# Encoder-side keys of a decoder block: K leaves PSUM once as fp32 with its halves made on GpSimd, value products stand in pairs, and the units of a batch in a new order

## The reference, cut to what matters

```python
# x (32, 56, 128), ctx_1024 (32, 1500, 128), 16 heads of 8
x = _layernorm(x + _L0_attn_ref(x, ...), axis=-1)
# cross-attention, q = x, k = v = ctx_1024
qh = (q @ Wq.T + bq).reshape(bs, -1, H, DK).transpose(0, 2, 1, 3)
kh = (k @ Wk.T + bk).reshape(bs, -1, H, DK).transpose(0, 2, 1, 3)
vh = (v @ Wv.T + bv).reshape(bs, -1, H, DK).transpose(0, 2, 1, 3)
scores = jnp.einsum('bhqd,bhkd->bhqk', qh, kh) / math.sqrt(DK)
attn = jax.nn.softmax(scores, axis=-1)
out = jnp.einsum('bhqk,bhkd->bhqd', attn, vh)
x = _layernorm(x + concat @ Wo.T + bo, axis=-1)
x = _layernorm(x + _L0_ffn_ref(x, ...), axis=-1)
```

## Time and profile before

| | us |
|---|---|
| median of 3 runs | 888.73 (888.48 to 889.25) |
| the profiled execution | 889.02 |
| its span, first to last instruction | 887.2 |
| first score of body 0 | at 133.01 |
| first score of body 1 | at 155.57 |
| first score of body 30 | at 797.01 |
| first score of body 31 | at 819.62 |

### The profile page before, as it was taken

How to read it: one execution, slowest core, us unless ns; L and a number is a source line. 1 busy time by engine, 2 the same in 40 slices (tenths; PEclk the granted TensorE clock), 3 DMA queues, 4 the chain that set the end, 5 groups by cost and what they waited for, 6 DMA issues and landing times.

```text
span 887.2 us, 28853 instructions
## 1 busy us (share of the span) xinstructions
PE 825.6 (93%) x11074; PEld 534.8 (60%) x11074; DVE 692.8 (78%) x1245; ACT 559.0 (63%) x759; POOL 294.3 (33%) x170
## 2 busy tenths in 40 slices
PE   6788669999999999999999999999999999998884
PEld 3555426666666666666666666666666666666553
DVE  7767687778787878787878787878787878788498
ACT  4566517666666666666666666666666666666863
POOL 6010524333333333333333333333333333300263
PEclk9989959999999999999999999999999999999898
DMA  6000044333333333333333333333333332222001
GB/s 201 1 10 21 21 129 105 92 86 90 86 87 87 86 88 87 87 86 88 85 87 88 86 86 88 87 87 89 85 92 82 93 84 78 52 53 55 1 1 42
DMA packets 29864, 67.37 MB, mean 76 GB/s; under 512 B 8072, under 2 KB 13192, under 8 KB 29704
## 3 DMA queue, kind: packets, MB, share of 16 engines
q1 hardware_dynamic: 29832, 66.94, 28.7%
HBM read 27.50 MB, written 0.92 MB: 32 GB/s over the span
## 4 chain that ended last, share of the span: by engine, by line
PE 73%; DVE 15%; ACT 5%; issue 5%; DMA 1%; DVEq 0%; POOL 0%; ACTq 0%
PE psum L807 19%; PE psum L846 16%; PE psum L831 14%; PE psum L800 6%; PE psum L794 6%; DVE r_sb L1112 5%; PE psum L851 4%; ACT kh L594 2%; PE psum L722 2%; DVE kl L1091 2%; PE psum L820 2%; PE psum L708 1%; DVE k_stack L1226 1%; DVE rden L1025 1%; DVE mx L1098 1%
## 5 line engine op out<-in xcount | busy, mean ns | idle before, releaser
L1098 DVE TENSOR_REDUCE mx<-psum 128x1 f32<-128x500 f32 x672 | 413.0, 672 | 52.7 <-PE psum L807 49.5
L576 ACT ACTIVATE probs<-psum 125x896 f32<-125x896 f32 x384 | 352.7, 919 | 149.9 <-PE psum L831 146.4
L807 PE MATMUL psum<-kh,q_max 128*128 128x500 f16 x672 | 234.5, 383 | 7.3 <-DVE mx L1098 2.0
L831 PE MATMUL psum<-q_diag,k_stack 97*128 97x224 f16 x1536 | 212.9, 261 | 2.7 <-DMA q_diag<-mT 1.8
L846 PE MATMUL psum<-probs,v_ext 125*32 125x168 f32 x3072 | 189.3, 319 | 1.2 <-ACT probs L576 1.2
L831 PEld LDWEIGHTS psum<-q_diag,k_stack 97*128 97x128 f16 x1536 | 140.7, 98 | 46.6 <-issue 16.9
L442 POOL CAST c_hl<-c_in 128x1500 f16<-128x1500 f32 x32 | 45.9, 1434 | 267.8 <-PE psum L800 261.9
L1091 DVE SCALAR_TENSOR_TENSOR kl<-psum,pack,kh 128x500 f16<-128x500 f32 x96 | 68.0, 735 | 83.4 <-ACT kh L594 83.4
L846 PEld LDWEIGHTS psum<-probs,v_ext 125*32 125x32 f32 x3072 | 60.6, 108 | 114.9 <-issue 97.2
L450 POOL TENSOR_TENSOR q_diag<-q_stack,pack 96x896 f16<-96x896 f32 (+1 forms) x32 | 54.2, 1693 | 171.0 <-PE psum L831 158.7
L851 PE MATMUL psum<-probs,v_ext 125*16 125x56 f32 x3072 | 108.4, 213 | 0.0
(11 more groups left out here) (143 smaller groups left out, 735.0 us busy)
## 6 DMA issues: line engine op xcount, KB each, us to landing
c_in<-ctx_in SPq DMA_DIRECT2D x32, 750.0 KB, 4.3
k_stack<-kh SPq DMA_DIRECT2D x256, 93.8 KB, 2.2
k_stack<-kl SPq DMA_DIRECT2D x128, 93.8 KB, 2.2
pack<-pack_in SPq DMA_DIRECT2D x1, 1107.0 KB, 5.9
q_stack<-qh SPq DMA_DIRECT2D x32, 32.0 KB, 1.8
out<-x_all SPq DMA_DIRECT2D x8, 112.0 KB
pack<-pack_in SPq DMA_DIRECT2D x1, 848.5 KB, 4.7
x_all<-x_in SPq DMA_DIRECT2D x2, 336.0 KB
```

The source lines that it names most:

```text
L576: nc.scalar.activation(probs[0:KP, t % PBUF, :].rearrange("p (a c) -> p a c", a=2), scores[t % 2][0:KP, :, 0:2 * GC], ACT.Exp, scale=SCALE ...
L807: last = nc.tensor.matmul(bank[:, 0:CH], q_max[u][:, r * P:(r + 1) * P], kh[:, c * CH:(c + 1) * CH], start=True, stop=True)
L831: last = nc.tensor.matmul(scores[t % 2][:, g // 2, (g % 2) * GC:(g % 2 + 1) * GC], k_stack[u][0:ROWS, g, t * KP:t * KP + P], q_diag[u][0:R ...
L1098: dve.tensor_reduce(mx[:, i:i + 1], bank[:, 0:CH], AX.X, ALU.max).then_inc(mx_done, 1)
```

## The change

- **K.** ACT writes K of a chunk once as fp32 to a new buffer k32 (k_copy), which frees the bank. POOL casts it to kh (kcast) and subtracts for kl (ksub), chunk by chunk. DVE's k_lo is gone. kh and kl now exist twice (u = 0, 1). SP's stack_k waits for kl as before.
- **POOL's order.** split works in three chunks, and takes batch b+2 in body b. A body on POOL is now: cast of the last chunk of b+1, split of b+2, subtraction of that chunk, q_max, q_diag, then cast and subtraction of the first two chunks of b+2.
- **Value products.** They come two at a time, every second step, for the two steps before. The last two of a batch stand in the next body. The 224 columns are cut into 112 and 112 (v_ext's columns 0 to 32 and 16 to 48), so two heads in each product; WoSlots, selB and R follow.
- **Units.** PLAN gives for each pair of steps what stands after the first score, after the second, and after the two value products. K of a batch is made in three places: chunks 0 and 1 in body b-2 (K2), chunk 2 in body b-1 (K1). M goes chunk by chunk rather than row by row (M_ORDER): the first 7 (chunk 0) in body b-2 (M2), the other 14 in body b-1 (M1). R, and with it the reciprocal, moves from step 0 to step 7, X from step 11 to the end of step 7; o_copy of b-1 goes to DVE's place ahead of step 2.
- **Ends.** Two K and seven M of batch 1 are made ahead of body 0. The split of batch 1 stands early in POOL's front part. The last bodies have no K2 and M2.
- The scratch that the program reserves for DMA descriptors is set to 1024, for the new buffers' room.

The core of the diff:

```diff
-M_COUNTS = (2, 2, 3, 2, 3, 2, 3, 2, 2)
-V_STEPS, Y_STEP = (0, 2, 4), 6
-X_STEP = 11
-TAIL = [("K", c) for c in range(KC)]
+EARLY_M = 7
+PLAN = ((("M1",), ("M1", "K1", "M1"), ("V", "M1", "V")),
...
+O_COPY = (1, -1)
...
-                def split(n, buf, half):
+                def split(n, buf, half, i):
...
+                    keys = slice(i * CH, (i + 1) * CH)
+                    nc.gpsimd.tensor_copy(c_hl[:, buf, 0, keys], c_in[:, buf, keys]).then_inc(c_hi, 1)
...
+                def kcast(n, i, u):
...
+                    pool.wait_ge(k32_done, n * KC + i + 1)
                     settle(pool, pool_settled)
+                    nc.gpsimd.tensor_copy(kh[u][:, i * CH:(i + 1) * CH], k32[:, i * CH:(i + 1) * CH]).then_inc(kh_done, 1)
+
+                def ksub(n, i, u):
...
+                    nc.gpsimd.tensor_tensor(kl[u][:, keys], k32[:, keys], kh[u][:, keys],
+                                            ALU.subtract).then_inc(kl_done, 1)
...
-                def k_hi(n, i, bank):
...
+                def k_copy(n, i, bank):
+                    act.wait_ge(ready["K"], n * KC + i + 1)
+                    wait_past(act, kl_done, (n - 1) * KC + i + 1)
+                    nc.scalar.activation(k32[:, i * CH:(i + 1) * CH], bank[:, 0:CH], ACT.Identity,
+                                         bias=w("bk")).then_inc(k32_done, 1)
...
+                    elif kind in ("M1", "M2"):
+                        r, c = M_ORDER[i]
+                        if i % MB == 0:
+                            pe.wait_ge(kh_done, n * KC + c + 1)
...
-                        nc.tensor.matmul(O[32 * j:32 * j + 32, 0:3 * N], v_ext[u][0:KP, t, j, 0:32],
-                                         probs[0:KP, t % PBUF, at:at + 3 * N], start=(t == 0), stop=(t == KT - 1),
+                        nc.tensor.matmul(O[32 * j:32 * j + 32, 0:2 * N], v_ext[u][0:KP, t, j, 0:32],
+                                         probs[0:KP, t % PBUF, at:at + 2 * N], start=(t == 0), stop=(t == KT - 1),
...
+                    for m, (one, two, three) in enumerate(plans[u]):
+                        score(b, 2 * m, u)
...
+                        go(one)
+                        score(b, 2 * m + 1, u)
+                        go(two)
+                        if m:
+                            pv(b, 2 * m - 2, u)
+                            pv(b, 2 * m - 1, u)
+                        elif before:
+                            pv(b - 1, KT - 2, 1 - u)
+                            pv(b - 1, KT - 1, 1 - u)
+                        go(three)
...
-                def k_lo(n, i, bank):
...
-                    dve.scalar_tensor_tensor(kl[:, i * CH:(i + 1) * CH], bank[:, 0:CH], w("bk"),
-                                             kh[:, i * CH:(i + 1) * CH], ALU.add, ALU.subtract).then_inc(kl_done, 1)
```

More of the change, by code:

```diff
@@ L508, in add_b2 @@
+                for b in range(B - 2, B):
+                    body(b, b // 2, b % 2, False, b + 1 < B)
                 def add_b2(q):
@@ L782, in _, with release @@
                 front(QUADS - 1, True, False)
-                def unit(kind, i, n, u, bank, before):
+                def release(before):
                     if before is not None:
@@ new lines, in of_batch, with body, go @@
+                def of_batch(kind, b, pair):
+                    return {"K2": b + 2, "M2": b + 2, "R": b - 1, "Y": pair - 1}.get(kind, b + 1)
+                def body(b, pair, u, s1, s2, before, held):
+                    held = dict(held)
+                    def go(units):
+                        for kind, i in units:
+                            if active(kind, s1, s2, before):
+                                n, slot = of_batch(kind, b, pair), slots[u][kind, i]
+                                if kind in ("M1", "M2") and i in PAIRS:
+                                    release(held[slots[u][kind, i + 1]])
+                                unit(kind, i, n, u if kind in ("K2", "M2") else 1 - u, ring[slot], held[slot])
+                                held[slot] = (kind, i, n)
+                    for m, (one, two, three) in enumerate(plans[u]):
+                        score(b, 2 * m, u)
+                        if not s2 and 2 * m in X2T_STEPS:
+                            x2_T(X2T_STEPS.index(2 * m))
+                        go(one)
[8 more added lines that the diff above has]
+                        go(three)
+                    if not s2:
+                        pv(b, KT - 2, u)
+                        pv(b, KT - 1, u)
@@ L1145, in _ @@
                 q_lo(QUADS - 1)
[L1146 to L1147 removed]
+                for i in range(EARLY_M):
+                    m_max(1, i, banks[early_bank("M1", i)])
                 dve.wait_ge(sin_done, 1)
@@ L1198, in body @@
                                 add_y(pair - 1, bank)
-                    for i in range(KC):
-                        if s1:
-                            k_lo(b + 2, i, ring[slots[u]["K", i]])
-                        if i == 0:
-                            o_copy(b, u)
+                    for m, parts in enumerate(plans[u]):
+                        if (m, -1) == O_COPY and before and s2:
+                            o_copy(b - 1, 1 - u)
+                        for part, units in enumerate(parts):
+                            reduce(units)
+                            if (m, part) == O_COPY and before and s2:
+                                o_copy(b - 1, 1 - u)
                 for b in range(2):
```

305 lines of the change are left out of this document (166 added, 139 removed).

## The result

| | before | after |
|---|---|---|
| median, us | 888.85 (888.48 to 889.25) | 841.27 (839.2 to 841.89) |
| profiled execution | 889.02 | 840.91 |
| its span | 887.2 | 838.9 |
| first score of body 0 | 133.01 | 133.54 |
| of body 1 | 155.57 | 158.00 |

The changed kernel takes 0.9461 of the time before [0.9443, 0.9478], 47.6 us less, inside the range and 3.7 us from the forecast. From the starts of the scores, the 48.3 us of span come from these places: bodies 1 to 29 take 595.59 in place of 641.44 us (-45.9), body 30 takes 18.9 in place of 22.6 (-3.7), the last body with the tail 66.4 in place of 67.6 (-1.2), and body 0 takes 24.5 in place of 22.6 (+1.9), behind a front that is 0.5 longer.

A forecast was written before the change was run, and what follows sets the result against it. PE's row of instructions was taken as the bound. 29 x (22.14 - 20.8) = 38.9 us from the bodies and 4.9 from body 30 make 43.8 us less, so 845 us, range 833 to 866.

The forecast's parts named there:

- What bounds the kernel: Main loop: a 22.14 us batch takes as long as PE's instructions stand in a row; only shortening that row helps.
- Pairs: Value products on PE: six pairs cost 6.0 us a batch against 7.3 for twelve single ones, gaining 1.3.
- K's halves on POOL: POOL's 500-column cast at 0.60 us and subtraction at 1.14; DVE losing three k_lo was worth nothing on the path.
- rival 3: GpSimd's pieces cost more, a subtraction about 1.45 us: 21.4 us a body, 862 us in all; chance 0.13.
- The chain to k_stack: From a body's first score through POOL (done at 10.3 us), SP's 12 copies and place_m: next body at 20.1 us.
- The chain to M2: POOL's cast for the early maximum products is ready at 14.4 us, PE comes at 14.5: just hidden.
- The wait on DVE: The small cast of the maxima waits 0.8 us for POOL's diag_q; PE then waits 0.5 us at the second M2.
- rival 1: No DVE wait, the small cast gets in at once: 20.4 us a body on average, 835 us; chance 0.17.
- Rivals 2 and 4: Small DVE cast gets in only at POOL's first gap, 862 us (0.14), or once POOL is really idle, 892 (0.04).
- Rival 5: Pairing doesn't save the switch, the second value product pays as the first: about 884 us; chance 0.02.
- The front and body 0: Start of the kernel: shorter cast wait and one K fewer against added work before the first score; 0, -3 to +3.
- Body 30: Next-to-last body, without M2 and K2: 17.7 us in place of 22.61, a gain of 4.9.

## Why the prediction was right, and where only the total was

**What bounds the kernel**: right as far as it went. PE's row is the bound before, and in even bodies after. But "only what shortens that row helps" is half of it: the pairs alone shorten the row, and the time went up by 7 us, because DVE's row in the middle of the old body is as long as PE's (3.0 for 3.1 us).

**Pairs**: the price was right to 0.01 us a pair (0.99 for 1.00), and the cut at nothing was right. What it left out is that the 1.3 us are had only if DVE can take maxima faster. I wrote that DVE idles a fifth of the time and that PE waits for nothing in its stead; that average hid the stretch from 431.18, eleven reductions in a row in the kernel before. Of the old order the sum would have given 855; the chip gave 896.5. The forecast held because the new order spreads the maxima, not because I had seen that it must.

**K's halves on POOL**: 0.60 and 1.14 were taken, 0.602 and 1.138 measured; rival 3 falls. The factor of 1.96 between GpSimd and DVE that stood beside that rival (the Trainium skill, GPSIMD Engine Reference, section Performance versus the Vector engine) is not what this size shows: DVE took 0.735 for its k_lo, POOL 1.138, a factor of 1.55 (the two read different sources).

**The chain to k_stack**: 10.3 us to the subtraction's end were predicted, 10.2 measured; 20.1 for the body, 20.12 measured, with 2.03 from place_m to the score as in the earlier trace rows. The written terms add up to 19.9, though (10.3, 7.6 and 2.03); the 0.2 between is what passes from the subtraction's end to SP's first copy (10.21 to 10.45). The run with a longer chain confirms the chain.

**The chain to M2**: PE at 14.5, measured 14.6 (543.12 less 528.55); cast done at 14.4, measured 14.05. Hidden by 0.5 rather than 0.1.

**The wait on DVE**: the mechanism was right and the size was wrong, and this is the step that failed. The cast came at 13.1, not 12.9, and q_diag ended at 13.5, not 13.7: 0.25 us of wait, not 0.8. The reciprocal then ended at 15.0 (543.54), ahead of the second M2 at 15.2, where the prediction had it at 15.5 behind a product at 15.0. So the 0.5 us a body weren't there, 29 x 0.5 = 14.5 us of the sum. The odd bodies' chain takes 15 x 0.25 = 3.8 of them back, and their long cases 3.0 (below); 0.6 more went because 29 x 22.14 is over the 641.44 us of before. That leaves the 7 us by which the bodies came out better than forecast. Even bodies are at 20.77, which is PE's row of 20.75 without the wait; odd ones fall on the chain at 20.1. Those are the bodies of rival 1 (20.4 on average), by another mechanism than its own: the cast did not get in at once. Rivals 2 and 4 fall with the row of 541.66: DVE gets its turn between two instructions of POOL that stand back to back. Rival 5 falls with the pair's 0.41.

**Why then 841 and not 835**: three terms were too low. The front and body 0 were put at 0 and cost 2.4: the cast of the maxima is indeed short now (0.17 for 2.53), but in body 0 POOL's row starts at 140.19, and PE pays for it with a wait of 1.41 ahead of M2 and 3 us at half the clock. The prediction had named the late start, "as it does now", and put it at nothing. Body 30 was put at 17.7 us and took 18.9: I had left out that it is an even body with Y at its end. And the odd bodies take 3.0 us more than 15 times 20.12, most of it in the first two, 21.43 and 21.13. POOL is on time in these; it is SP's queue that is late, with 4.07 and 3.41 us for the four kl copies rather than 2.50:

```profile
173.24 4.07 SPq L381 DMA_DIRECT2D k_stack<-kl  x4
```

Why the copies take longer there is open. The last body with the tail gave 1.2 us where 0 to 1 of loss was taken. Bodies 45.9 for 38.9 predicted, ends 2.4 for 4.9: two errors of opposite sign, 7.0 and 2.5 us. They leave 4.5 of the span, and 3.7 between the forecast and the median, which flatters the working. And by its own sign, a wait of PE of more than 1 us in a body, the prediction was wrong in bodies 0, 1 and 3 (1.41 ahead of M2, then 1.7 and 1.2 for place_m).

## What to carry over

Before pricing a faster row on the bounding engine, look for the stretch in which its consumer already works without a gap, not at the consumer's average: there the saving needs a new order as well, and neither pays alone. When a chain is taken off the path, read what PE then waits for first; here it was the bank that the table of slots reused at once. A short VectorE instruction beside long GpSimd ones is priced by where it falls in the one in flight, so it is worth a row of its own in the sum, with both ends kept.

## What the runs showed of the hardware

- A VectorE cast of 7 columns waits for the end of the GpSimd instruction in flight, and as a rule no longer: 0.17 us alone, a median of 0.47 in the changed kernel, 0.44 with one more long instruction queued behind, and 1.61 where it comes just as one begins. Four times, within 0.05 us of a boundary, it waited for the whole of the next one, 1.72 to 1.73. That it gets in between two GpSimd instructions without a gap was not expected.
- Two value products in four column groups cost the same at 168 and 56 columns as at 112 and 112: 0.41 us from one to the next, 0.91 for two, though the records give 312 and 213 ns for the one cut, 266 and 260 for the other. For the 0.22 us that a single one pays for the change from full-array products and back, the Trainium skill, TensorEngine Tiling (Array Packing), section Key Properties, says that a change of tiling mode drains the engine; the trace agrees that there is a cost.
- An edit on one engine moves the wait to where slack had hidden it: 0.1 us gained in odd bodies came back as 0.26 in even ones.
- TensorE's granted clock was 0.50 in body 0 from 153 to 155, after PE had been busy for 1.0 of the 3.1 us from 148.0 to 151.1, and 0.50 for 5.7 us behind the wait of 3.27 in the run with the later q_stack; over bodies 1 to 29, where PE's longest wait was 1.7 us, it was 1.00.
